# Causal attention with batches of one 384-key block, diagonal blocks only where a query may look, and paired maxima eight batches ahead

## The reference

```python
q = q.reshape(B, T, NUM_HEADS, D_HEAD)
...
scale = 1.0 / np.sqrt(D_HEAD)
logits = jnp.einsum('bqhd,bkhd->bhqk', q, k) * scale
causal = jnp.tril(jnp.ones((T, T), dtype=bool))
logits = jnp.where(causal, logits, jnp.finfo(logits.dtype).min)
attn = jax.nn.softmax(logits, axis=-1)
attn_out = jnp.einsum('bhqk,bkhd->bqhd', attn, v).reshape(B, T, D)
```

## Time and profile before

| what | value |
|---|---|
| median of 3 runs | 5769.16 us (5764.76 to 5770.94) |
| the profiled execution's own time | 5774.45 us |
| its span, first to last instruction | 5772.7 us |
| PE busy over the span | 5223.8 us (90%) |
| DVE, ACT, POOL busy | 3456.3, 2394.0, 3087.8 us |
| mean granted TensorE clock | 0.947 |

### The profile page before, as it was taken

How to read it: one execution, slowest core, us unless ns; L and a number is a source line. 1 busy time by engine, 2 the same in 40 slices (tenths; PEclk the granted TensorE clock), 3 DMA queues, 4 the chain that set the end, 5 groups by cost and what they waited for, 6 DMA issues and landing times. The chain is left out here.

```text
span 5772.7 us, 84105 instructions
## 1 busy us (share of the span) xinstructions
PE 5223.8 (90%) x23692; PEld 3069.8 (53%) x23692; DVE 3456.3 (60%) x4336; ACT 2394.0 (41%) x5287; POOL 3087.8 (53%) x1607
## 2 busy tenths in 40 slices
PE   8799999999999999999997896999979889887970
PEld 4456555555555555555554444565545555554540
DVE  3477776767767677776775445555434444452228
ACT  3255555555555555555554121333323333332420
POOL 0089899898999989999897011555540000000001
PEclk9799999999999999999998888999989999998985
DMA  6511111111111111111112565022220000001121
GB/s 222 182 44 44 26 38 37 44 44 37 35 30 44 44 39 31 38 38 44 39 30 70 139 181 145 24 60 61 61 70 11 22 16 22 22 11 40 49 111 51
DMA packets 244613, 330.97 MB, mean 57 GB/s; under 512 B 87260, under 2 KB 224754, under 8 KB 234490
## 3 DMA queue, kind: packets, MB, share of 16 engines
q1 hardware_dynamic: 244218, 326.08, 20.2%
HBM read 202.49 MB, written 123.51 MB: 56 GB/s over the span
## 5 line engine op out<-in xcount | busy, mean ns | idle before, releaser
L658 POOL TENSOR_TENSOR diff_run_pool<-diff_run_pool,diff_probs 128x768 f32<-128x768 f32 x1152 | 2249.9, 1953 | 113.5 <-ACT diff_probs L506 24.8
L586 DVE TENSOR_REDUCE diff_maxes<-diff_max 128x1 f32<-128x768 f32 x1752 | 1571.1, 950 | 726.4 <-PE diff_max L408 725.4
L506 ACT ACTIVATE diff_probs<-diff_ring 128x384 f32<-128x384 f32 x3462 | 1399.0, 495 | 866.2 <-PE diff_ring L398 856.1
L434 PE MATMUL diff_out_ps<-diff_probs,diff_vs 128*64 128x384 f32 x6912 | 1253.1, 498 | 0.0
L398 PE MATMUL diff_ring<-diff_qs,diff_ks 97*128 97x384 f32 x3462 | 1074.3, 384 | 17.7 <-issue 9.3
L408 PE MATMUL diff_max<-diff_ks,diff_qs 96*128 96x384 f32 x3504 | 948.2, 352 | 39.2 <-DMA diff_vs<-v_rows 31.7
L398 PEld LDWEIGHTS diff_ring<-diff_qs,diff_ks 97*128 97x128 f32 x3462 | 606.1, 188 | 546.0 <-issue 355.1
L434 PEld LDWEIGHTS diff_out_ps<-diff_probs,diff_vs 128*64 128x64 f32 x6912 | 447.9, 137 | 546.6 <-issue 343.0
L2091 POOL MEMSET pick_before<- 128x128 f32 x1 | 0.2, 204 | 1310.5 <-POOLq L63 1310.5
L408 PEld LDWEIGHTS diff_max<-diff_ks,diff_qs 96*128 96x128 f32 x3504 | 609.6, 192 | 82.2 <-issue 32.5
L1307 DVE TENSOR_REDUCE causal_maxes<-causal_max 128x1 f32<-128x384 f32 x522 | 281.0, 552 | 317.2 <-PE causal_max L1185 191.7
(11 more groups left out here) (230 smaller groups left out, 6039.5 us busy)
## 6 DMA issues: line engine op xcount, KB each, us to landing
diff_qs<-qk_hi SPq DMA_DIRECT2D x68, 288.0 KB, 4.3
diff_ks<-qk_hi SPq DMA_DIRECT2D x68, 288.0 KB, 6.0
diff_recip<-row_factors SPq DMA_DIRECT2D x194, 96.0 KB, 2.7
o_rows<-diff_normed SPq DMA_DIRECT2D x97, 192.0 KB, 1.9
qk_hi<-proj_hi SPq DMA_DIRECT2D x12, 1536.0 KB, 5.8
qk_lo<-proj_lo SPq DMA_DIRECT2D x12, 1536.0 KB, 9.6
causal_qa<-qk_hi SPq DMA_DIRECT2D x120, 96.0 KB, 2.5
diff_qs<-qk_lo SPq DMA_DIRECT2D x34, 288.0 KB, 5.3
```

Source lines behind the costliest of these rows:

```text
L434: mm = pe.matmul(out_ps[VD * j:VD * (j + 1), 0:T], vs[par][:, g, j, :], probs[g % PBUF][:, j * T:(j + 1) * T], start=g == 0, stop=g == STE ...
L506: act.activation(probs[g % PBUF][:, j * T:(j + 1) * T], ring[bank][:, 0:T], ACT.Exp, scale=SCALE).then_inc(s_taken, 1)
L586: dve.tensor_reduce(maxes[side][:, row:row + 1, h], max_ps[u % 2][:, :, 0:T], AX.XY, ALU.max).then_inc(s_red, 1)
L658: pool.tensor_tensor(run_pool[:], acc[:], probs[g % PBUF][:], ALU.add).then_inc(s_accp, 1)
```

## The change

The function is written anew. What it does:
- The unit of work is a batch, one block of 384 keys for one chunk: three steps. There are 84 batches, and the loop over images is gone: all four turns are written out.
- In batch order PE computes the six scores of batch e + 1 (three banks in a ring, which the rows and sums now share), among them up to three pairs of maxima, then all V products of batch e in one run, then a chunk's sums.
- On the diagonal, blocks are cut to what a query may see: scores, exponentials, sums and V products of the second and third block have 256 and 128 queries; maxima of the first and second third of the queries have 128 and 256 keys. The mask is added by a bf16 matmul of 128 columns.
- A pair of maxima is both heads' for one third of the queries, in one PSUM tile of two banks, taken by one DVE instruction. Two such tiles are in turn. Pairs run eight batches ahead (LEAD), so the first 24 pairs stand ahead of the first score. Nothing is computed for a third image.
- The transposed maxima are f32r matmuls against a broadcast column, and ACT copies both rows. ACT also copies the sums out of PSUM, and DVE inverts the copy.
- The probabilities have nine buffers in place of six, and outputs, sums and running sums two each.

The core of the diff, with "..." where lines are left out:

```diff
--- before.py
+++ after.py
@@ -984,69 +984,62 @@
     BANKS = 3
-    PBUF = 6
+    BATCH = SUB
+    PBUF = 3 * BATCH
+    NEGS = 4
+    LEAD = NC + 2
...
-    plan = [([], [], []) for _ in range(LAP)]
-    pair_steps, ahead = first[NC], len(units[0]) + len(units[1])
-    for z in range(SLOTS):
-        par, c = divmod(z, NC)
-        n = ufirst[NC] - ahead
-        for u in range(len(units[z])):
-            k = ufirst[z] - par * ufirst[NC] + u
-            if c < 2:
-                at = (par - 1) * pair_steps + first[NC - 1] + k * (steps[NC - 1] - 2) // ahead
-            else:
-                at = par * pair_steps + (k - ahead) * (first[NC - 1] - 1) // n
-            lap = 1 if at < 0 else 0
-            plan[at % LAP][0].append((lap, z, u))
-        plan[at % LAP][1].append((lap, z))
-        plan[(at + 1) % LAP][2].append((lap, z))
-        assert at + 1 < first[z]
...
+    first = [sum(z % NC + 1 for z in range(y)) for y in range(CHUNKS + 1)]
+    batches = [(z, k) for z in range(CHUNKS) for k in range(z % NC + 1)]
+    pairs = [(z, k, s) for z in range(CHUNKS) for k in range(z % NC + 1) for s in range(SUB)]
+    TOTAL = len(batches)
+    rows_at = {first[z] - 2: z for z in range(2, CHUNKS)}
+    ends_at = {first[z + 1]: z for z in range(CHUNKS)}
+    turned_at = {first[z + 1] + 1: z for z in range(CHUNKS)}
...
+    def place(tile):
+
+        e, i = divmod(tile, BATCH)
+        z, k = batches[e]
+        diagonal = k == z % NC
+        return z, BATCH * k + i, diagonal, i * P if diagonal else 0
+
+    def pairs_in(e):
+        return range(BATCH * (e + LEAD), min(BATCH * (e + LEAD + 1), len(pairs)))
...
-        probs = [sb(f"probs{i}", [P, 2 * T]) for i in range(PBUF)]
-        run_sum = sb("run_sum", [P, 2 * T])
-        row_sum = sb("row_sum", [P, 2 * T])
-        maxes = [sb(f"maxes{i}", [P, 2 * SUB, NC]) for i in range(2)]
-        neg_max = sb("neg_max", [P, 2 * SUB])
-        out_sb = sb("out", [P, T])
+        probs = [sb(f"probs{i}", [P, 2, T]) for i in range(PBUF)]
+        run_sum = [sb(f"run_sum{i}", [P, 2, T]) for i in range(2)]
+        maxes = [sb(f"maxes{i}", [P, 2, SUB, NC]) for i in range(2)]
+        neg_max = [sb(f"neg_max{i}", [P, 2, SUB], F32R) for i in range(NEGS)]
+        out_sb = [sb(f"out{i}", [P, T]) for i in range(2)]
+        sums_sb = [sb(f"sums{i}", [P, T]) for i in range(2)]
...
+                def score(tile, j):
+                    z, g, diagonal, lo = place(tile)
+                    turn, c = divmod(z, NC)
+                    if g == 0 and j == 0:
+                        pe.wait_ge(s_taken, slot["row", z, 1] + 1)
+                    keys, queries = slice(g * P, (g + 1) * P), slice(c * T + lo, (c + 1) * T)
+                    bank = free(slot["score", tile, j])
+                    pe.matmul(bank[:, lo:T], ka[turn % 2][j][:, keys], qa[j][:, queries], start=True, stop=False)
+                    mm = pe.matmul(bank[:, lo:T], kb[turn % 2][j][:, keys], qb[j][:, queries], start=False,
+                                   stop=not diagonal)
+                    if diagonal:
+                        mm = pe.matmul(bank[:, lo:lo + P], ident_bf[:], mask_k[:], start=False, stop=True)
+                    mm.then_inc(s_ring, 1)
...
+                    diagonal = k == c
+                    n = (s + 1) * P if diagonal else T
+                    queries, keys = slice(c * T + s * P, c * T + (s + 1) * P), slice(k * T, k * T + n)
...
+                        to = max_ps[u % 2]
+                        pe.matmul(to[:, j, 0:n], qa[j][:, queries], ka[turn % 2][j][:, keys], start=True, stop=False)
+                        mm = pe.matmul(to[:, j, 0:n], qb[j][0:TOP, queries], kb[turn % 2][j][0:TOP, keys],
+                                       start=False, stop=not diagonal)
+                        if diagonal:
+                            mm = pe.matmul(to[:, j, s * P:n], ident_bf[:], mask_q[:], start=False, stop=True)
                     mm.then_inc(s_mx, 1)
...
+                def rows(z):
+                    pe.wait_ge(s_neg, z + 1)
...
+                        bank = free(slot["row", z, j])
+                        for s in range(SUB):
+                            mm = pe.matmul(bank[:, s * P:(s + 1) * P],
+                                           neg_max[z % NEGS][:, j, s:s + 1].broadcast_to([P, P]), ident_r[:],
+                                           start=True, stop=True)
+                        mm.then_inc(s_ring, 1)
+                def pv_batch(e):
+                    z, k = batches[e]
+                    if k == 0 and z > 0:
+                        pe.wait_ge(s_oev, z)
+                    for tile in range(BATCH * e, BATCH * e + BATCH):
+                        _, g, _, lo = place(tile)
+                        pe.wait_ge(s_taken, slot["score", tile, 1] + 1)
+                        for j in range(2):
+                            mm = pe.matmul(out_ps[DH * j:DH * (j + 1), lo:T], vs[z // NC % 2][:, g, j, :],
+                                           probs[tile % PBUF][:, j, lo:T], start=g == 0,
+                                           stop=g == SUB * (z % NC + 1) - 1, tile_position=(0, DH * j))
...
+                for u in range(BATCH * LEAD):
+                    max_pair(u)
                 for z in range(2):
-                    for u in range(len(units[z])):
-                        max_unit(0, z, u)
-                    rows(0, z, 0)
-                with pe.Fori(0, B) as b:
-                    for at, (z, g) in enumerate(at_step):
-                        todo, _, made = plan[at]
-                        n = 1 if len(todo) > 2 else 0
-                        for lap, uz, u in todo[:n]:
-                            max_unit(b + lap, uz, u)
-                        score_step(b, z, g)
-                        for lap, uz, u in todo[n:n + 1]:
-                            max_unit(b + lap, uz, u)
-                        if g > 0:
-                            pv_step(b, z, g - 1)
-                        for lap, uz, u in todo[n + 1:]:
-                            max_unit(b + lap, uz, u)
-                        for lap, rz in made:
-                            rows(b + lap, rz, b * SLOTS + sums_before(at))
-                        if z > 0 and g == sums_step(z):
-                            sums(b, z - 1)
-                        if g == steps[z] - 1:
-                            pv_step(b, z, g)
-                    sums(b, SLOTS - 1)
+                    rows(z)
+                for e in range(-1, TOTAL):
+                    us = pairs_in(e) if e >= 0 else range(0)
+                    for i in range(BATCH):
+                        if e + 1 < TOTAL:
+                            for j in range(2):
+                                score(BATCH * (e + 1) + i, j)
+                        if i < len(us):
+                            max_pair(us[i])
+                    if e in rows_at:
+                        rows(rows_at[e])
+                    if e >= 0:
+                        pv_batch(e)
+                    if e in ends_at:
+                        sums(ends_at[e])
+                sums(CHUNKS - 1)
...
+                def take_sums(z):
+                    at = slot["sum", z]
+                    act.wait_ge(s_ring, at + 1)
+                    if z >= 2:
+                        act.wait_ge(s_norm, z - 1)
+                    act.activation(sums_sb[z % 2][:], ring[at % BANKS][:, 0:T], ACT.Copy).then_inc(s_taken, 1)
...
+                def max_pair(u):
+                    z, k, s = pairs[u]
+                    n = (s + 1) * P if k == z % NC else T
+                    dve.wait_ge(s_mx, u + 1)
+                    dve.tensor_reduce(maxes[z % 2][:, :, s, k], max_ps[u % 2][:, :, 0:n], AX.X, ALU.max
+                                      ).then_inc(s_red, 1)
...
+                count = 0
+                for tile in range(BATCH * TOTAL):
+                    z, g, _, lo = place(tile)
+                    acc = run_sum[z % 2]
+                    if g == 0 and z % NC > 0:
+                        continue
+                    pool.wait_ge(s_taken, slot["score", tile, 1] + 1)
+                    if g == (0 if z % NC == 0 else 1) and z >= 2:
+                        pool.wait_ge(s_ring, slot["sum", z - 2] + 1)
+                    if count > 0:
+                        pool.wait_ge(s_acc, count)
+                    if g == 0:
+                        pool.tensor_copy(acc[:], probs[tile % PBUF][:]).then_inc(s_acc, 1)
+                    elif g == 1 and z % NC > 0:
+                        pool.tensor_tensor(acc[:], probs[(tile - 1) % PBUF][:], probs[tile % PBUF][:], ALU.add
+                                           ).then_inc(s_acc, 1)
+                    else:
+                        pool.tensor_tensor(acc[:, :, lo:T], acc[:, :, lo:T], probs[tile % PBUF][:, :, lo:T], ALU.add
+                                           ).then_inc(s_acc, 1)
+                    count += 1
```

354 lines of the change are left out of this document (149 added, 205 removed).

## The result

| | before | after |
|---|---|---|
| median (range, runs) | 5770.05 us (5764.76 to 5777.49, 4) | 5627.49 us (5617.24 to 5631.36, 4) |
| span of the profiled execution | 5772.75 us | 5628.77 us |
| first maximum to first score | 16.58 us | 27.41 us |
| first score to end of the last sums | 714.93 us | 560.47 us |
| the whole stage, first maximum to last product | 734.73 us | 591.61 us |

The account below looks back on a forecast made before the run. TensorE's own pace was taken as the bound. Differences 1 to 7 gave -148.5 us and 4 us fewer waits made it 152, so 5769 - 152 = 5617 us; 8-in-10 range 5600 to 5650.

Parts of the forecast that it names:

- The bound: Causal loop: TensorE's own pace, priced by distances between starts, sets the time; prices sum to 700 of 715 us, 15 waits.
- Item 1: V products three steps at a time: 168 fewer pairs of precision changes at 0.345, -58.0 us; sums following them, -4.1.
- Item 2: Masks as one 128-column matmul each, taken at 0.07 us: 288 x 0.107, -30.8 us.
- Item 3: Diagonal blocks cut to 384, 256 and 128 columns: cheaper scores, maxima and V products, -39.3 us.
- first rival: Narrow diagonal blocks give nothing, 256 f32r columns going as two passes: +18, masks +14, about 5640 us; chance 0.13.
- Item 4: Transposed maxima in the loop: 0.63 us in place of 0.97, 22 in place of 24, -9.4 us.
- Item 5: Loop's second lap no longer recomputes maxima for nobody; 48 fewer units in the loop, -17.0 us.
- Item 6: Ahead of the loop: 24 pairs of maxima, mostly paced by DVE, first score 26 us after the start, +9.4 us.
- The end: Last eight batches: POOL is slower than PE, nine buffers hold its lag, and it ends some 1 us after PE.
- Item 7: Behind the last sums: ACT copies them ahead of the three reciprocals, +0.7 us.
- Waits elsewhere: TensorE's waits in the loop: 3 us at the start, 2 in the last eight batches, 5 spread.
- Batches that wait as in the differential stage: Rival: the ring of three banks waits for ACT, 0.25 us a batch, +21, about 5638 us; chance 0.15.

## Why the prediction was right, point by point

- **The bound.** TensorE's pace by starts, with 15 us of waits, carried over: the full batch came out at 6.518 against 6.52 (2.12 + 2.12 + 1.93 + 0.345), and a batch's V products on the diagonal are 0.640 shorter, forecast 0.645.
- **Item 1, precision changes.** 0.345 a pair forecast, 0.35 measured in full batches with the products put back.
- **Item 2, masks: mis-sized.** I took 0.07 between bounds of 0 and 0.177; leaving them out shows 0.101, so 288 x 0.031 = 9 us of the gain were not there. Among 128-column neighbours a mask does cost 0.075 (0.30 from mask to mask, less two places of 0.112), among wider ones 0.12 to 0.13. My guess started from the mask's own columns, and it should have been priced like any 128-column matmul (0.105 to 0.11 in the earlier trace rows).
- **Item 3, narrow blocks.** 0.12 at 256 columns and 0.112 at 128, as taken. The Trainium skill's 81 ns for a load and 128 columns ("TensorE: Matmul & The Clock Gate", Back-to-back issue gap) does not appear in these f32r rows. By the forecast's prices, with 0.101 for masks, full width costs 39.3 + 288 x 0.076 = 61.2; measured 56.7, of which the shorter end explains 1.1. One sum of the first rival is off: 5617 + 18 + 14 is 5649, not "about 5640".
- **Item 4, rows.** By starts in the trace after, a chunk's rows put the V products 0.62 later, and 0.67 behind a mask; forecast 0.63.
- **Item 5, the 48 units computed for nobody** (17.0), the rows (9.4) and the sums (4.1) stand on counts and pitches. No run puts them back. The two runs that put parts back, V products by step and full width, account for 109 of the 143 us if the two add, which no run tests either.
- **Item 6, the prologue.** 27.4 us, forecast 26. DVE paced it as said: six reductions of 768 in 5.95.
- **The end: mis-sized.** "It ends some 1 us after PE" was 5.0. The forecast's own prices, 5.5 for POOL and 4.4 for PE, let POOL lag by 1.1 us in each full batch of the last chunk; I did not add that up, and nothing supports the 1 us. POOL's timeline has no gap from there on:

```profile
4102.61 29.78 POOL L1371 TENSOR_TENSOR causal_run_sum<-causal_run_sum,causal_probs 128x768 f32<-128x768 f32 x16
```

  With the clock's fall behind that wait (0.7), 6.5 us lie between the last V product and the end of the last sums, of which 2 were forecast: 4.5 too few. Item 7, the tail behind the sums, was charged with 0.7 and grew by 0.5 (3.73 instead of 3.22).
- **Waits elsewhere: mis-sized the other way.** Some 10 us were charged (3 at the start, 2 in the last eight batches, 5 spread). The trace shows 0.95 for ACT in the first batch, and in each of the seven periods without maxima 0.29 (4.69 instead of 4.40), 2.0 in all. In the other batches of the loop the trace has no wait of PE's. So 7 of the 10 were not there. With 8.4 for the 270 masks in the loop and 4.5 at the end, the loop should be 6 longer than forecast; it is 7.5 longer, and the prologue 1.4. The remaining 1.6 I can't place. Errors of opposite sign hid a part of each other, and that the total came within 9 us is partly luck.
- **Not named in the forecast: the edge between the images.** In PE's timeline before, the second lap of the loop begins so:

```profile
3920.91 0.68 PE L1184 MATMUL causal_max<-causal_ka,causal_qa 128*128 128x384 f32 x1 [3.72 <-issue]
```

  PE had waited 1.09 us for POOL ahead of the last sums, then stood idle for 3.72 with no releaser in the profile, and its granted clock was 0.50 up to 3924.1, with matmuls 0.32 apart instead of 0.177 (1.5 us longer, an estimate from these distances). These 6 us are a part of what the forecast had as 15 us of waits. With all four turns written out, the trace after has no such edge; no run separates this gain.
- **Covers.** POOL in the loop, ACT and DVE never set the pace: in the loop PE never waits for DVE. The products with the reciprocals have a median of 0.906 us instead of 0.558, against "the operation is the same after"; nothing waits for it.
- **The rivals.** Batches that wait as in the differential stage: not where maxima lie between the scores (6.518), but the seven periods without maxima do just that, 4.69 as against 4.66 there. They wait more when a score is held back by its neighbour's mask. The clock in the loop stayed at 1.00 until 4129.9.

## What to carry to other kernels

Price TensorE by the distance between starts, at every width and at every change of precision, and group what shares a precision: a pair of changes between fp32 and f32r cost 0.35 us here, two f32r matmuls of 384 columns' worth. A small f32r matmul pays more for a place than for its columns (0.112 us at 128, 0.120 at 256, 0.177 at 384), so put small ones of one kind side by side, unless that holds back a bank for which the next engine waits. Where the work of one engine dries up at the end (maxima, here), work out again who is the slowest from there on: POOL's lag showed only in the last 30 us of the loop. Look at the granted clock before you explain a difference of a microsecond or two by waits.

## What I had not expected of the hardware

- A lone bf16 mask of 128 columns costs as much as an f32r one (0.36 from mask to mask with two 256-column matmuls, in both). The starts behind it are uneven in both, 0.04 and 0.21 for bf16, 0.07 and 0.17 for f32r; why is open. Two bf16 masks in a row save 0.061.
- After an idle stretch of 5.0 us TensorE came back at its lower clock level: four fp32 records took 1.54 us, and 0.81 where it had gone on working. In two runs, masks side by side and maxima in two reductions, it fell to that level in the first batch too, behind waits of only 1.10 and 0.95 us. The length of the wait alone does not decide it: in the other ten profiled executions of the changed kernel and its variants PE waited 0.36 to 1.28 us in the same place, and the clock stayed at 1.00.
- A POOL copy of 768 values a partition is far cheaper than its addition of the same size (1.83). By tile:

```profile
L1366 POOL COPY causal_run_sum<-causal_probs x4: 824/824/825, 3576.5 to 3999.6; 128x768 f32<-128x768 f32 x4
L1327 DVE TENSOR_TENSOR causal_normed<-causal_out,causal_recip x24: 557/906/1956, 3598.1 to 4137.3; 128x384 f32<-128x384 f32 x24
```

The second row is the product whose median rose. Its form and engine are those of before; what differs is when it starts. In both traces it takes 0.56 us when no addition of POOL's is running at its start (or one that ends within 0.01 us), also when one starts 0.04 us later. When one is running, the product ends 0.41 us after that addition does: 8 of the 24 products before (1.08 or 2.17 us) and 15 of the 24 after (most 0.98, one 1.96).
